# Experts' weights issued by ScalarE, a third down product held, and the next-to-last group's ranks moved behind the last up product

## The reference

```python
xt = layernorm(x).reshape(b * s, d)
scores = sigmoid(xt @ gate_w.T)                       # 8 experts
top_scores, top_idx = top_k(scores, 2)                # divided by their sum, times 2.5
combine = sum(one_hot(top_idx, 8) * top_scores[..., None], axis=1)
y = einsum("eth,ehd->etd", silu(xt @ w1[e]) * (xt @ w3[e]), w2)
routed = einsum("etd,te->td", y, combine)
shared = silu(xt @ sw1) * (xt @ sw3) @ sw2            # hidden width 352
out = x + (routed + shared).reshape(b, s, d)
```

## Time and profile before

| | us |
|---|---|
| median of three executions | 1528.33 |
| lowest, highest | 1523.52, 1529.8 |
| the profiled execution, its own time | 1535.9 |
| its span in the trace | 1534.0 |
| TensorE busy (share of the span) | 1414.4 (92%) |
| VectorE busy | 893.3 (58%) |
| ScalarE busy | 508.8 (33%) |
| GpSimd busy | 452.3 (29%) |

### The profile page before, as it was taken

One profiled execution on the slowest core, in us unless ns is written; L12 is line 12 of the kernel. 1 busy time (PEld: TensorE's weight loads), 2 busy tenths in 40 slices (PEclk: granted clock), 3 DMA queues, 4 the chain that ended last, 5 costly groups with the idle time before them and its releaser, 6 DMA issues.

```text
span 1534.0 us, 21932 instructions
## 1 busy us (share of the span) xinstructions
PE 1414.4 (92%) x6059; PEld 704.4 (46%) x6060; DVE 893.3 (58%) x2655; ACT 508.8 (33%) x1042; POOL 452.3 (29%) x431
## 2 busy tenths in 40 slices
PE   6997999999999998899899984699999999999996
PEld 3552223333433332455455542355555555555553
DVE  4898998888788861678687864233333333333331
ACT  4662456766676677212021121011111111111110
POOL 0000000000000000000222252667777777777771
PEclk9996999999999999899899997799999999999998
DMA  7685310310320000466676752244444444444442
GB/s 219 217 237 156 80 39 4 78 43 5 68 58 4 5 5 16 135 195 180 158 174 176 180 101 50 48 67 71 69 69 69 69 69 69 69 70 70 69 69 35
DMA packets 124854, 136.81 MB, mean 89 GB/s; under 512 B 37046, under 2 KB 86590, under 8 KB 124774
## 3 DMA queue, kind: packets, MB, share of 16 engines
q1 hardware_dynamic: 101350, 96.56, 24.4%
q0 software_dynamic: 21520, 37.84, 14.4%
q10 hardware_dynamic: 1904, 1.46, 0.3%
HBM read 87.03 MB, written 48.83 MB: 89 GB/s over the span
## 4 chain that ended last, share of the span: by engine, by line
PE 72%; DVE 13%; DMA 5%; issue 5%; ACT 2%; SPq 1%; POOL 1%; ACTq 0%; DVEq 0%; POOLq 0%
PE psum L1046 28%; PE psum L1057 14%; PE psum L959 8%; PE psum L941 7%; PE psum L923 6%; PE psum L873 3%; DVE arena L1239 3%; DVE psum L1237 2%; PE psum L1029 2%; DMA xq<-xn_rows 2%; DMA xn_rows<-xg 2%; DMA attn_cur<-attn_rows 1%; PE psum L1020 1%; PE psum L944 1%; ACT arena L709 1%
## 5 line engine op out<-in xcount | busy, mean ns | idle before, releaser
L1046 PE MATMUL psum<-arena,xg_t 128*128 (+2 forms) x1648 | 520.1, 470 | 20.5 <-DVE xg_t L1209 19.9
L1046 PEld LDWEIGHTS psum<-arena,xg_t 128*128 128x128 f32 x1648 | 312.4, 195 | 182.8 <-issue 32.9
L781 ACT ACTIVATE arena<-psum 128x512 f32<-128x512 f32 (+3 forms) x640 | 303.6, 535 | 176.2 <-PE psum L941 87.3
L643 POOL DMA_INDIRECT table<-const,slot_i x64 | 62.5, 976 | 865.2 <-DVE slot_i L1424 756.1
L659 POOL DMA_INDIRECT xq<-xn_rows,quad_rows x284 | 272.2, 958 | 96.4 <-issue 88.9
L1057 PE MATMUL psum<-arena,act_t 128*128 (+3 forms) x618 | 282.5, 593 | 1.2 <-ACT act_t L809 0.7
L1239 DVE TENSOR_REDUCE arena<-psum 128x1 f32<-128x512 f32 x384 | 251.0, 685 | 30.5 <-PE psum L923 29.9
L923 PE MATMUL psum<-arena 96*128 96x512 bf16 (+3 forms) x640 | 219.1, 363 | 17.8 <-DVE arena L1237 9.6
L1320 DVE TENSOR_TENSOR act_sb<-psum,silu 128x352 f32<-128x352 f32 x103 | 54.0, 524 | 284.8 <-ACT silu L831 226.9
L941 PE MATMUL psum<-arena 99*128 99x512 bf16 (+3 forms) x640 | 215.0, 353 | 3.5 <-ACT arena L781 2.7
L831 ACT ACTIVATE silu<-psum 128x352 f32<-128x352 f32 x103 | 47.8, 464 | 466.8 <-PE psum L1046 410.5
(11 more groups left out here) (138 smaller groups left out, 894.6 us busy)
## 6 DMA issues: line engine op xcount, KB each, us to landing
arena<-qk_parts SPq DMA_DIRECT2D x48, 256.0 KB, 6.2
arena<-in_w SPq DMA_DIRECT2D x16, 704.0 KB
arena<-in_x SPq DMA_DIRECT2D x32, 256.0 KB, 4.4
x<-in_x SPq DMA_DIRECT2D x32, 256.0 KB
xn_rows<-xg SPq DMA_DIRECT2D x32, 256.0 KB
xq<-xn_rows SPq DMA_DIRECT2D x128, 64.0 KB
out_rows<-y_sb SPq DMA_DIRECT2D x32, 256.0 KB
qk_parts<-arena SPq DMA_DIRECT2D x16, 384.0 KB, 3.2
```

The lines of the kernel that those rows point to most:

```text
L781: nc.scalar.activation(probs[:, at_b % PS, d * P:], psum[:, NA + at_b % NBK, 0:CH - d * P], ACT.Exp, scale=float(HD) ** -0.5).then_inc(s_e, 1)
L1046: i = nc.tensor.matmul(psum[:, bank + k % 2, 0:w], xg_t[:, k % 2, c, :], rhs, start=c == 0, stop=c == DC - 1)
```

## The change

- The 32 DMAs of the experts' weights move from SyncE to ScalarE. The last two parts of an expert become one ("whole parts": 24 parts of 704 KB, the third of each expert issued as two DMAs). They are spread over steps 0 to 27 (one at most per step, none in step 0), behind the copy of the activations' transposes and ahead of the sigmoid and silu. ScalarE first waits for attention's last stores and mask loads, as the weights overwrite their buffers.
- The ranks of group 4 move from the head of step 31 to behind its up products, and VectorE's slots of group 4 to behind the gating of tile 31.
- The down products of tiles 29 and 30 leave the step loop and stand, with that of 31, behind the last up product: `act_t` gets a third buffer, and tiles 29 and 31 use PSUM bank 7. VectorE's y of tiles 29 and 30 leave the loop too.
- The constant table for the block list has 71 columns in place of 568, read as a broadcast. The constants loaded at the start shrink by 497 of their 845 columns of four bytes in each of 128 partitions, by 254 KB.

```diff
-for _n, _w in (("ident", P), ("rev8", E), ("first_slot", E), ("iota_be", NB * E), 
+for _n, _w in (("ident", P), ("rev8", E), ("first_slot", E), ("iota_b", NB), 
...
-COUNT_AT = {12: 0, 20: 1, 27: 2, 29: 3, 31: 4}
+COUNT_AT = {12: 0, 20: 1, 27: 2, 29: 3}
+HELD = 3
+W_STEPS = 28
...
-        act_t = sb("act_t", [P, 2, HC, P])
+        AT = HELD
+        act_t = sb("act_t", [P, AT, HC, P])
...
             def shared(n, k):
...
                 if k < NT - 2:
                     store_xn2(n + 2, k + 2)
-                load_expert(n // 4, n % 4)
                 if k < NT - 2:
                     load_quarters(n + 2, k + 2)
...
+            for i in range(2):
+                act.wait_ge(s_mld[i], 16 * NS // 2)
+                act.wait_ge(s_ast[i], 16 * NS // 2)
+
+            def load_expert(e, part):
+
+                if part < 2:
+                    act.dma_start(w13[:, e, :, part * H:(part + 1) * H],
+                                  (w1_rows, w3_rows)[part][e * D:(e + 1) * D, :].rearrange("(c p) n -> p c n", p=P)).then_inc(s_w, 16)
+                if part == 2:
+                    act.dma_start(w2[:, e, 0:HC - 1, :],
+                                  w2_rows[e * H:e * H + (HC - 1) * P, :].rearrange("(c p) n -> p c n", p=P)).then_inc(s_w, 16)
+                    act.dma_start(w2[0:HL, e, HC - 1, :], w2_rows[e * H + (HC - 1) * P:(e + 1) * H, :]).then_inc(s_w, 16)
...
-                    if k >= 2:
-                        act.wait_ge(ss["dn"], n - 1)
-                    nc.scalar.copy(act_t[:, k % 2], psum[:, 5, 0:HP].rearrange("p (c n) -> p c n", c=HC)).then_inc(ss["ate"], 1)
+                    if k >= ring:
+                        act.wait_ge(ss["dn"], n - ring + 1)
+                    nc.scalar.copy(act_t[:, k % ring], psum[:, 5, 0:HP].rearrange("p (c n) -> p c n", c=HC)).then_inc(ss["ate"], 1)
...
                         at_copy(n - 1, k - 1)
                     if ss is sh:
+                        for i in range(3 * E * n // W_STEPS, min(3 * E, 3 * E * (n + 1) // W_STEPS)):
+                            load_expert(i // 3, i % 3)
...
                 def down(n, k, e):
                     pe.wait_ge(ss["ate"], n + 1)
+                    held = shared and n >= NT - HELD
 
                     if k >= 1:
-                        pe.wait_ge(ss["ye"], n)
+                        pe.wait_ge(ss["ye"], n - 1 if held else n)
+                    out = psum[:, 7 if held and (NT - n) % 2 == HELD % 2 else 6, :]
...
                     up(n, k, expert(n))
-                    if k >= 1:
+                    if k >= 1 and not (shared and n - 1 >= NT - HELD):
                         down(n - 1, k - 1, expert(n - 1))
...
+                    ranks(len(GROUPS) - 2, NT)
+                    down(NT - 3, NT - 3, None)
+                    at(NT - 1, NT - 1)
+                    down(NT - 2, NT - 2, None)
+                    ranks(len(GROUPS) - 1, NT)
+                    down(NT - 1, NT - 1, None)
...
                         if k < count - 1:
                             turn(n + 1, k + 1)
+                        if n == count - 1:
+                            slots(len(GROUPS) - 2)
                         for g, part in CHOOSE.get(n, ()):
                             choose(g, part)
-                    if k >= 1:
+                    if k >= 1 and not (shared and n - 1 >= NT - HELD):
                         y(n - 1, k - 1)
...
                     choose(len(GROUPS) - 1, 2)
                     slots(len(GROUPS) - 1)
+                    y(NT - 3, NT - 3)
                     block_list()
+                    y(NT - 2, NT - 2)
...
-                chain(nc.vector.tensor_tensor(by_block, over_b(ends), cf("iota_be").rearrange("p (b e) -> p b e", e=E), ALU.is_le))
+                chain(nc.vector.tensor_tensor(by_block, over_b(ends), cf("iota_b").rearrange("p (b a) -> p b a", a=1).broadcast_to([P, NB, E]), ALU.is_le))
```

More of the change, by code:

```diff
@@ L71, in constants @@
     put("first_slot", (np.arange(E) * T)[None])
-    put("iota_be", np.repeat(np.arange(NB), E)[None])
+    put("iota_b", np.arange(NB)[None])
     put("quarter", np.arange(P)[:, None] // QW)
@@ L572, in store_y @@
                 sp.dma_start(rows(dst, n), y_sb[:, k % 2, :]).then_inc(ss[f"stored_{k % 2}"], 16)
[L574 to L583, removed]
             def shared(n, k):
@@ L1050, in down @@
                     pe.wait_ge(ss["ate"], n + 1)
+                    held = shared and n >= NT - HELD
                     if k >= 1:
-                        pe.wait_ge(ss["ye"], n)
+                        pe.wait_ge(ss["ye"], n - 1 if held else n)
+                    out = psum[:, 7 if held and (NT - n) % 2 == HELD % 2 else 6, :]
+                    ring = AT if shared else 2
                     for c in range(HC):
@@ L1056, in down @@
                         rhs = sh2[0:r, c, :] if shared else w2[0:r, bass.ds(e, 1), c, :].rearrange("p a n -> p (a n)")
-                        i = nc.tensor.matmul(psum[:, 6, :], act_t[0:r, k % 2, c, :], rhs, start=c == 0, stop=c == HC - 1)
+                        i = nc.tensor.matmul(out, act_t[0:r, k % ring, c, :], rhs, start=c == 0, stop=c == HC - 1)
                     i.then_inc(ss["dn"], 1)
@@ L1079, in experts @@
                         step(n, n)
+                    ranks(len(GROUPS) - 2, NT)
[4 more added lines that the diff above has]
+                    down(NT - 1, NT - 1, None)
                 else:
                     run_steps(pe, count, step, u)
-                at(count - 1, count - 1)
-                if shared:
-                    ranks(len(GROUPS) - 1, NT)
-                down(count - 1, count - 1, expert(count - 1))
+                    at(count - 1, count - 1)
+                    down(count - 1, count - 1, expert(count - 1))
             def ranks(g, turns):
@@ L1334, in y @@
                     if shared:
-                        i = nc.vector.tensor_tensor(y_sb[:, k % 2, :], x1[:, k % XR, :], psum[:, 6, :], ALU.add)
+                        bank = 7 if n >= NT - HELD and (NT - n) % 2 == HELD % 2 else 6
+                        i = nc.vector.tensor_tensor(y_sb[:, k % 2, :], x1[:, k % XR, :], psum[:, bank, :], ALU.add)
                     else:
@@ L1445, in block_list @@
                 chain(nc.vector.scalar_tensor_tensor(block_slot, eid, float(T // P), start, ALU.mult, ALU.subtract))
-                chain(nc.vector.tensor_tensor(block_slot[0:1, :], block_slot[0:1, :], cf("iota_be")[0:1, :].rearrange("p (b e) -> p b e", e=E)[:, :, 0], ALU.add))
+                chain(nc.vector.tensor_tensor(block_slot[0:1, :], block_slot[0:1, :], cf("iota_b")[0:1, :], ALU.add))
                 chain(nc.vector.tensor_scalar(start_i[:, :], block_slot[0:1, :], float(QW), None, ALU.mult))
```

1 line of the change is left out of this document (added).

## The result

The change makes the kernel slightly slower: 1530.5 us, median of 20 executions (1525.44 to 1536.64), against 1525.53 for the kernel before (20 executions, 1522.8 to 1532.72). The ratio is 1.0031, with a 95% interval from 1.0018 to 1.0045, about 5 us. I had forecast 8 us less.

The account below looks back on a forecast made before the run. TensorE was taken as the bound almost everywhere, but not in the shared expert's stage, tiles 24 to 31. Gains of 3.5 + 2.0 + 1.0 + 1.8 = 8.3 us take the median from 1528.33 to 1520.0 us, range 1511 to 1530.

Parts of the forecast that it names:

- Ranks moved: End of shared stage: tile 31's up products start at 926.80 instead of 930.37, not waiting for group 4's ranks; 3.5 us gained.
- Three held down products: Behind tile 31's up products: other work covers the down products moved there; cost 0, up to 5.5 us without that cover.
- Quarters of tile 31 sooner: SyncE's quarter loads for tile 31 no longer stand behind weights in one queue; 2.0 us gained, between 0 and 5.2.
- The clock: Tile 31's up products: a shorter wait ahead may keep TensorE's clock from falling; 1.0 us gained, 2.4 at most.
- The other stalls: Scatter steps: weights issued early are mostly through before the stall, shortening TensorE's gaps of 6.56 and 7.17 us; 1.8 us gained.
- ScalarE's issues: Shared stage: two weight issues of 0.45 us each fit where ScalarE idles 4.31 us ahead of the silu; cost 0.
- Constants: Kernel start: 254 KB less to load, 1.2 us at most, but the first product waited for other weights; taken as 0.
- routed stage: Stage of the routed blocks after the shared expert: same order as before, so a change of 0.
- Slower: Rival, shared stage: ScalarE's weights enter slow stretches after scatters and share DMA engines with quarters and attention tiles; up to 1544.5; chance 0.10.
- Only the order counts: Rival: scatters cause the slow stretches whoever issues weights, so only 3.5 us of gain remain, 1524.8; chance 0.22.

Follow-up runs that it names:

- whole_parts_only: Kernel before with only the weights' pace changed: 24 whole parts over steps 0 to 27, SyncE behind the store; 1526.08 us against 1528.37, ratio 0.9985.
- tail_only: Changed kernel with the weights back on SyncE behind the store in 32 parts; 1525.53 us, ratio 0.9985 to the kernel before.
- tail_two_held: As `tail_only`, but two down products held instead of three; 1519.37 us against 1524.81 for the kernel before, ratio 0.9966.
- tail_whole_parts: Changed kernel with its 24 whole parts issued by SyncE behind the store; 1516.25 us against 1524.81 before, ratio 0.9955; repeated: 1523.96 us, ratio 0.9968.
- const_only: Kernel before with only the block list's table cut to 71 columns and read as a broadcast; 1528.14 us against 1528.19, ratio 1.0.
- queue_only: Kernel before with only the weights moved to ScalarE as the change does, 24 whole parts over steps 0 to 27; 1538.61 us, ratio 1.0079.
- queue_old_pace: As `queue_only`, but in the old 32 parts, one per step in steps 0 to 31; 1539.69 us, ratio 1.007 to the kernel before.
- queue_behind_silu: As `queue_only`, but ScalarE issues the weights behind the silu, about when SyncE did before; 1539.74 us, ratio 1.0086 to the kernel before.
- queue_after_store: As `queue_behind_silu`, but ScalarE first waits until the store of tile n + 2 has landed; 1544.69 us, ratio 1.0104 to the kernel before.

## Why the prediction was wrong

**Ranks moved, 3.5 us: right as a mechanism.** The 7.65 us wait of the earlier trace rows for ranks is 1.28, and the ranks stand behind up(31). What the tail as a whole brings is 2 to 5 us, by the ratios 0.9985, 0.9966 and the two with whole parts against `whole_parts_only`; 3.5 lies within it. `tail_only` by itself is not clear of noise (0.9966 to 1.0004).

**Three held down products, 0: right as far as the medians tell.** Slots of group 5 came 6.67 us behind up(31), forecast 6.8; first routed block 28.4 us behind it in both. No run shows that the third product held is of use. It may have a price that I did not see: with the down product of tile 29 gone from ahead of up(31), TensorE has less to do there, and up(31) took 6.45, 6.53, 7.66 and 7.82 us in the four profiles with three held. In both with two held it took 5.05:

```profile
918.43 5.05 PE L1051 MATMUL psum<-arena,xg_t 128*128 128x360 f32 x16 [1.77 <-DVE xg_t L1220]
```

That is `tail_two_held`. By the medians two and three held are not told apart.

**Quarters of tile 31 sooner, 2.0 us: the size right, the reason in part.** From the last quarter issue to the transpose it was 3.4 us (920.27 to 923.67), 5.6 before, so 2.2 us less. They were used 5.15 us after their first issue, where I wrote under 5. With no weights in its last steps, the store still took 5.0 us (913.49 to 918.52), against 6.4 in the earlier trace rows. From the store to the transpose it was 10.2 us, 14.4 before. But in `tail_whole_parts`, where SyncE issues and the weights likewise end at step 27, these are 4.9 and 10.4 us, and in `tail_only`, where SyncE issues weights there, 6.2 and 13.4. So the gain comes from ending the weights early, not from ScalarE. `whole_parts_only` prices the early end and the whole parts together at 0.9985, 2 us.

**The clock, 1.0 us: not shown.** Up(31) took 6.45 us against 7.31, not near 5. But 6.45 to 7.82 us in kernels with the same tail, and 6.71 and 6.11 in `const_only` and `whole_parts_only` without it, say that the 0.9 us of this pair can be chance. The window that answers to the earlier trace rows, granted clock behind the busy times:

```profile
920.00:940.00 20.00, 14.48 (x48) 7.83 (x47) 12.03 (x65) 4.91 (x8) 4.56 (x5) 0.91 0.12 27
```

0.91 in place of 0.74, so less of the stretch at 1.2 GHz, and not none.

**The other stalls, 1.8 us gained: the step that failed.** The prediction said that ScalarE issues at the start of a step and SyncE in its last third, "so in scatter steps weights are mostly through before the stall", and that early weights therefore help the stores and loads behind them. In scatter steps they do the opposite: in 765 to 880 us SyncE waits 55.1 us for its stores, against 19.9 and 25.0 in `tail_whole_parts` and its repeat, where nothing differs but that SyncE issues the weights behind the store, and TensorE is busy 104.3 us of the 115, against 111.4 and 109.1. That in a normal step the weights are through before the store was nearly true (2.0 to 2.8 us in place of 2.0 to 2.2), and of no help. The term was not a gain of 1.8 but a loss. Its size comes from three pairs that differ in the place of the weights and share their pace and tail: 1.0079 against 0.9985 (`queue_only`, `whole_parts_only`), 1.0031 against 0.9955 and 0.9968 (the change, `tail_whole_parts` twice), 1.007 against 1 (`queue_old_pace`, before). Those are 10 to 14 us lost, where I had put 1.8 gained.

The gap of tile 17 did shrink, from 6.56 to 2.99 us, as I had written, and so did that at tile 28, from 7.17 to 4.71. That says nothing of the weights: at the place of the first, 745 to 758 us, one profile of `tail_whole_parts` has two gaps of 1.92 and 1.43 us and that of its repeat one of 6.37, with SyncE issuing in both, and `queue_only` has 6.24. These were the two places I had looked at. The loss came in many others, where before there was mostly no wait to see:

```profile
PE psum L1021 <- DMA attn_cur<-attn_rows: 9.3, 7, 3.0
```

That is TensorE in 725 to 915 us after, seven waits against two before; in `queue_only` there are seven also, 14.5 us in all, against 6.4 in `whole_parts_only`. "New waits of TensorE for attention tiles in steps 12 to 23" stood in the text as what would prove me wrong.

**ScalarE's issues, 0: right.** One takes 0.37 to 0.48 us, and ScalarE goes on waiting for TensorE ahead of its silus. **Constants, 0** and **routed stage, 0**: right (`const_only` 1.0; 567.5 us against 567.9).

**The rivals.** "Slower" had the mechanism: weights that go out whatever the DMA engines do, in steps 12 to 29, share them with quarters and attention tiles. I gave it 0.10, 0.09 of it over half a per cent, and priced it by whole gaps of 6.56 us; in the changed kernel it is many small ones. With 10 to 12 us, by the pairs with its own pace and tail, it takes back the 5 to 7 us of the tail and the early end of the weights and leaves +5. The rule cited for "Only the order counts", from the Trainium skill ("DMA: Bandwidth & Descriptors", Rules for kernel authors), that spreading DMAs over issuing engines only saves issue time, was nearer than my sum: nothing was saved by the second queue. The rule names no harm, and here 0.7 to 0.9% was lost (`queue_old_pace`, `queue_only`, `queue_behind_silu`), by where the bulk loads stand beside the round trip.

The other rule that the prediction cites, from the Trainium skill ("DMA: Bandwidth & Descriptors", Queues, rings and completion order), that a semaphore write lands only after all earlier writes of its DMA engine, across queues, fits these rows: 4.01 us for a store with weights 0.12 us ahead of it in another queue, 2.15 with weights 0.36 us behind it. Plain sharing of the DMA engines would lengthen the store too, and no run tells the two apart. By the rule my term should have been negative and not 0, for the change moved the weights from behind the store to ahead of it. I had applied it to one half only.

**What stays open.** Why `queue_after_store` still waits 79.4 us in the scatter steps, when its undisturbed stores are as quick as before, was not settled. Its weights stand close ahead of the next store there, but slow stores without them occur as well; a version in which ScalarE's wait holds nothing behind it was not tried. Nor do the runs say whether the stores, the quarter loads or the attention tiles behind the weights cost TensorE the time, since every edit moved all of them against the weights. Nor was it shown by itself how much of the slow stretches of the earlier trace rows is the scatters' own. Every kernel has them.

## What to carry to other kernels

Before a bulk load is moved to an idle engine's queue, look at what it stood behind: right behind a store whose landing its queue waits for was the best of the five places tried here; put ahead of the store, in either queue, it lengthened the round trips, most of all in steps with scatters. Why the place behind the store is cheap was not shown; my reading is that the DMA engines work on the bulk in just that wait. Price such an edit over all the steps, not by the two largest gaps of the trace, and look where the bound engine has slack: in 640 to 725 us longer round trips cost nothing. And let the medians of many executions decide over a difference of half a per cent, since two single profiles here had the sign wrong.

## What the hardware showed that I had not expected

- A 256 KB store's round trip, without scatters, depends on half a microsecond of issue order: 2.15 us with 704 KB issued 0.36 us behind it (2.0 to 2.2 in all such steps), 4.01 us with them 0.12 us ahead in another queue (3.0 to 4.9), 3.44 us with them 3.9 us ahead in the same queue (2.0 to 3.6 with weights 2.2 to 4.0 us ahead).
- A scatter right behind the store need not slow it: 2.28 us at 781.11, with the scatter at 781.23 and weights at 781.47, where the store of the earlier trace rows, in the first scatter steps, took 8.0 us.
- The same program differs in one execution from the next by more than the change: the 20 executions of the kernel before lie between 1522.8 and 1532.72 us, the change is 5.
